# Where the steps that bring expert results home stand in a software pipeline

## The reference, cut to what matters

```python
x = _layernorm(x + linear_attention(x))          # softplus features, causal cumulative sums
x = _layernorm(x + cross_attention(x, ctx))      # 16 heads of 64, keys from 120 context rows and x
# the last sublayer, experts:
scores = softmax(x @ gate_w.T); topk_w, topk_i = top_k(scores, 2)      # 2 of 8 experts for each token
topk_w = topk_w / topk_w.sum(-1) * 2.5
y = sum over the two experts e of topk_w * (silu(x @ w_gate[e]) * (x @ w_up[e])) @ w_down[e]   # width 176
shared = (silu(x @ sw_gate) * (x @ sw_up)) @ sw_down                   # width 352, every token
x = _layernorm(x + y + shared)
```

## Time and profile before

| | us |
|---|---|
| median of 3 runs | 2102.3 (2101.9 to 2102.84) |
| the profiled execution's own time | 2103.97 |
| its span, first to last instruction | 2102.1 |
| PE, DVE, ACT, POOL busy | 1959.1, 1527.5, 1259.2, 1338.7 |
| mean granted TensorE clock | 0.974 of full |

### The profile page before, as it was taken

How to read it: one execution, slowest core, us unless ns; L and a number is a source line. 1 busy time by engine, 2 the same in 40 slices (tenths; PEclk the granted TensorE clock), 3 DMA queues, 4 the chain that set the end, 5 groups by cost and what they waited for, 6 DMA issues and landing times. The chain is left out here.

```text
span 2102.1 us, 47412 instructions
## 1 busy us (share of the span) xinstructions
PE 1959.1 (93%) x15991; PEld 1697.7 (81%) x15991; DVE 1527.5 (73%) x4030; ACT 1259.2 (60%) x3812; POOL 1338.7 (64%) x1475
## 2 busy tenths in 40 slices
PE   6888859999999999999999999999999989999874
PEld 4555448999999999999999999998999877888763
DVE  5999946777777777777777777778777755555554
ACT  4565526666666666666666666666666644444453
POOL 5899937566666666666666666666666664444564
PEclk9999969999999999999999999999999999999976
DMA  5200000000000000000000000001000022322344
GB/s 141 58 18 18 16 25 6 9 14 22 16 17 14 22 15 17 15 18 17 18 15 14 21 17 15 15 21 33 19 15 14 21 60 75 85 73 74 96 141 120
DMA packets 105022, 75.78 MB, mean 36 GB/s; under 512 B 11044, under 2 KB 98676, under 8 KB 104660
## 3 DMA queue, kind: packets, MB, share of 16 engines
q1 hardware_dynamic: 93732, 53.66, 9.4%
q0 software_dynamic: 8640, 17.97, 2.5%
q10 hardware_dynamic: 2416, 1.12, 0.2%
HBM read 40.15 MB, written 32.57 MB: 35 GB/s over the span
## 5 line engine op out<-in xcount | busy, mean ns | idle before, releaser
L1026 POOL TENSOR_TENSOR x_prob<-x_prob,x_inv 128x496 f32<-128x496 f32 x514 | 521.8, 1015 | 464.2 <-DVE x_inv L1176 461.7
L1104 ACT ACTIVATE x_prob<-x_ps_S,x_nmax 128x248 f32<-128x248 f32 x1028 | 472.8, 467 | 225.7 <-DVE x_nmax L1170 223.8
L1170 DVE TENSOR_REDUCE x_nmax<-x_ps_S 128x2 f32<-128x496 f32 x515 | 345.0, 670 | 106.0 <-PE x_ps_S L848 98.2
L1118 ACT COPY x_probT<-x_ps_T 124x512 f32<-124x512 f32 x512 | 300.3, 587 | 166.8 <-PE x_ps_T L1358 164.2
L846 PE MATMUL x_ps_S<-x_kT_lo,x_G_hi 128*128 128x248 f32 x1030 | 328.9, 319 | 0.0
L1358 PE MATMUL x_ps_T<-ident,x_prob 128*124 128x128 f32 x2048 | 319.4, 278 | 7.8 <-POOL x_prob L1026 6.3
L1358 PEld LDWEIGHTS x_ps_T<-ident,x_prob 128*124 128x124 f32 x2048 | 233.5, 140 | 74.0 <-POOL x_prob L1026 30.0
L848 PE MATMUL x_ps_S<-x_kT_hi,x_G_hi 128*128 128x248 f32 x1030 | 286.1, 278 | 0.0
L847 PE MATMUL x_ps_S<-x_kT_hi,x_G_lo 128*128 128x248 f32 x1030 | 286.0, 278 | 0.0
L1328 PE MATMUL x_ps_O<-x_probT,x_V 124*64 124x128 f32 x4096 | 251.9, 276 | 0.4 <-ACT x_probT L1118 0.4
L1585 POOL DMA_INDIRECT sorted_results<-e_y,w_wkv x142 | 145.1, 1022 | 164.9 <-DVE e_y L1717 153.4
(11 more groups left out here) (239 smaller groups left out, 4478.7 us busy)
## 6 DMA issues: line engine op xcount, KB each, us to landing
w_wkv<-sorted_rows SPq DMA_DIRECT2D x142, 66.0 KB
e_back<-sorted_results SPq DMA_DIRECT2D x28, 256.0 KB, 3.7
x_nk<-latents SPq DMA_DIRECT2D x34, 124.0 KB
latents<-lin_nlat SPq DMA_DIRECT2D x32, 128.0 KB, 1.8
turned_rows<-w_rows SPq DMA_DIRECT2D x32, 128.0 KB, 1.7
w_wq<-turned_rows SPq DMA_DIRECT2D x32, 128.0 KB
out_dram<-e_result SPq DMA_DIRECT2D x16, 256.0 KB, 2.8
x_nk<-in_ctx SPq DMA_DIRECT2D x34, 120.0 KB, 2.3
```

Of the source, the lines that this page charges most:

```text
L1026: nc.gpsimd.tensor_tensor(prob[:, k], prob[:, k], inv[:, k].unsqueeze(2).broadcast_to([P, 2, K]), ALU.mult).then_inc(prob_ready, 1)
L1104: nc.scalar.activation(prob[:, k, h, :], ps_S[:, n % BANKS, h * K:(h + 1) * K], ACT.Exp, bias=nmax[:, k, h:h + 1], accum_out=total[:, k, h ...
L1118: nc.scalar.copy(probT[0:KT, s % (2 * GANG)], ps_T[0:KT, s % 2, :]).then_inc(probT_ready, 1)
L1170: nc.vector.tensor_reduce(nmax[:, k, :], ps_S[:, n % BANKS, 0:2 * K].rearrange("p (h k) -> p h k", h=2), AX, ALU.max, negate=True).then_in ...
```

## The change

In `experts`:
- `add_pair` of group g moves to iteration 112 + 3g for g = 0 to 11 (12 groups in the block loop, not 9), and to 155, 157, 159 and 161 for groups 12 to 15. All loops are lengthened to STEPS_ALL = 170 iterations, and nothing is left behind them.
- SP's `load_back` of groups 0 to 11 moves to iteration 107 + 3g (five before `add_pair`; it was eight before), and SP's store to eight after `add_pair`. Groups 12 and 13 are loaded by SP in iteration 147, 14 and 15 by ACT in iteration 153.
- DVE's statistics are split over two iterations (`add_back`, `moments`), ACT's normalising over two (`normalise(g, pair)`). The addition of epsilon goes from POOL to DVE; POOL's power (`root`) stands in another iteration than `add_pair`, and ahead of it in the order.
- The shared groups 14 and 15 take seven iterations each from t = 143.

In `cross_attention` POOL makes the constants ahead of the first context rows.

```diff
-            for n in range(2):
-                context_deviation(n)
...
             nc.gpsimd.iota(ids[:], [[B * S, 2], [S, B]], base=0, channel_multiplier=1).then_inc(set_ready, 1)
...
             nc.gpsimd.tensor_tensor(before[:], tri[:], ident[:], ALU.subtract).then_inc(set_ready, 1)
+            for n in range(2):
+                context_deviation(n)
...
-    FIRST_BACK = FIRST_BLOCK[1] + 11
-    BACK_EVERY = 3
-    BACK = 9
+    LATE_FROM = TOTAL + 1
     WHOLE = FIRST[1] // GROUP
+    BACK_TIME = [FIRST_BLOCK[1] + 9 + 3 * g if g < WHOLE else TOTAL + 13 + 2 * (g - WHOLE) for g in range(GROUPS)]
+    STEPS_ALL = BACK_TIME[-1] + 9
...
+        def back_at(t, *delays):
+            for g, start in enumerate(BACK_TIME):
+                if t - start == delays[g >= WHOLE]:
+                    return g
+            return None
...
-                g = back_at(t + 8, 0)
-                if g is not None:
+                g = back_at(t, -5, -5)
+                if g is not None and g < WHOLE:
                     if g == 0:
                         sent_after(sp, FIRST_BLOCK[1])
                     for c in range(2):
                         load_back(sp, g, c)
-                g = back_at(t, 7)
+                if t == TOTAL + 5:
+                    sent_after(sp, TOTAL)
+                    for g in (WHOLE, WHOLE + 1):
+                        for c in range(2):
+                            load_back(sp, g, c)
+                g = back_at(t, 8, 7)
                 if g is not None:
                     store(g)
...
                 if 0 <= i < TOTAL:
                     scatter(i)
-                for delay, what in ((0, add_pair), (3, deviation)):
-                    g = back_at(t, delay)
-                    if g is not None:
-                        what(g)
+                g = back_at(t, 4, 3)
+                if g is not None:
+                    root(g)
+                g = back_at(t, 0, 0)
+                if g is not None:
+                    add_pair(g)
...
+                if t == TOTAL + 11:
+                    sent_after(act, TOTAL)
+                    for g in (WHOLE + 2, WHOLE + 3):
+                        for c in range(2):
+                            load_back(act, g, c)
```

More of the change, by code:

```diff
@@ L1074, in _ @@
             nc.gpsimd.tensor_tensor(before[:], tri[:], ident[:], ALU.subtract).then_inc(set_ready, 1)
+            for n in range(2):
+                context_deviation(n)
+                for u in range(2):
+                    normalise_context(n, n, u)
+                if n == 0:
+                    keys_hi(0, 0)
+                    keys_lo(0, 0)
             for k in range(2):
@@ L1456, in experts @@
         mom = room.sbuf("mom", [P, DEEP, GROUP, 2])
-        vare = room.sbuf("vare", [P, GROUP])
+        vare = room.sbuf("vare", [P, DEEP, GROUP])
         rstd = room.sbuf("rstd", [P, DEEP, GROUP])
@@ L1504, in shared_at, with prepared_at @@
         def shared_at(t):
-            g, k = divmod(t - SHARED_FROM, PIECES)
-            return (g, k) if 0 <= g < GROUPS else (None, None)
-        def back_at(t, delay):
-            g, rest = divmod(t - delay - FIRST_BACK, BACK_EVERY)
-            return g if rest == 0 and 0 <= g < BACK else None
+            if t >= LATE_FROM:
+                g, k = divmod(t - LATE_FROM, PIECES - 1)
+                g += GROUPS - LATE
+            else:
+                g, k = divmod(t - SHARED_FROM, PIECES)
+                if g >= GROUPS - LATE:
+                    return None, None
+            return (g, k) if 0 <= g < GROUPS else (None, None)
+        def prepared_at(t):
+            starts = [SHARED_FROM + PIECES * g for g in range(GROUPS)]
+            return starts.index(t) if t in starts else None
+        def back_at(t, *delays):
[3 more added lines that the diff above has]
+            return None
         @block.sync
@@ L1539, in _ @@
             slots.store_turned(sp, LAST)
-            for t in range(TOTAL + 4):
+            for t in range(STEPS_ALL):
                 if t % SET == 0 and t + RING < TOTAL:
                     load_rows(t // SET + LOADS)
-                g, k = shared_at(t + 13)
-                if g is not None and g > 1 and k == 0:
+                g = prepared_at(t + 13)
+                if g is not None and g > 1:
                     load_all(g)
@@ L1593, in add_pair, with root @@
                                         ).then_inc(pair_ready, 1)
-            def deviation(g):
+            def root(g):
                 wait(pool, shift_ready, g - DEEP + 1)
-                wait(pool, rstd_ready, g)
-                pool.wait_ge(mom_ready, (g + 1) * GROUP)
-                nc.gpsimd.tensor_scalar(vare[:], mom[:, g % DEEP, :, 1], EPS, None, ALU.add).then_inc(vare_ready, 1)
                 pool.wait_ge(vare_ready, g + 1)
-                nc.gpsimd.tensor_tensor(rstd[:, g % DEEP], vare[:], slots.half[:], ALU.pow).then_inc(rstd_ready, 1)
-            for t in range(TOTAL + 4):
+                nc.gpsimd.tensor_tensor(rstd[:, g % DEEP], vare[:, g % DEEP], slots.half[:], ALU.pow).then_inc(rstd_ready, 1)
+            for t in range(STEPS_ALL):
                 i = t - 3
@@ L1653, in all_gate, with normalise @@
                                      ).then_inc(all_silu_ready, 1)
[L1655 to L1659, removed]
+            def normalise(g, pair):
+                if pair == 0:
+                    act.wait_ge(shift_ready, g + 1)
+                    wait(act, stored[g % DEEP], g // DEEP * 16)
+                for k in (pair * 2, pair * 2 + 1):
                     nc.scalar.activation(result[:, g % DEEP, k, :], hsum[:, g % DEEP, k, :], ACT.Identity,
@@ L1671, in _ @@
                 g, k = shared_at(t)
-                if g is not None and g < GROUPS - LATE and k < NS:
+                if g is not None and k < NS:
                     all_gate(g, k)
-                g, k = shared_at(t + 2)
-                if g is not None and k == 0:
+                g = prepared_at(t + 2)
+                if g is not None:
                     all_hi(g)
@@ L1680, in _ @@
                     slots.scores_of(act, LAST)
[L1681 to L1692, removed]
+                for pair in range(2):
+                    g = back_at(t, 6 + pair, 5 + pair)
+                    if g is not None:
+                        normalise(g, pair)
+                if t == TOTAL + 11:
[3 more added lines that the diff above has]
+                            load_back(act, g, c)
         @block.vector
@@ L1749, in add_back, with moments @@
                 dve.wait_ge(sum_ready, g + 1)
-                for k in range(GROUP):
+                for k in range(2):
+                    v.bn_stats(stat[:, k, :], hsum[:, g % DEEP, k, :]).then_inc(stat_ready, 1)
+            def moments(g):
+                for k in range(2, GROUP):
                     v.bn_stats(stat[:, k, :], hsum[:, g % DEEP, k, :]).then_inc(stat_ready, 1)
@@ L1754, in add_back @@
                     v.bn_aggr(mom[:, g % DEEP, k, :], stat[:, k, :]).then_inc(mom_ready, 1)
+                dve.wait_ge(mom_ready, (g + 1) * GROUP)
+                wait(dve, rstd_ready, g - DEEP + 1)
+                v.tensor_scalar(vare[:, g % DEEP], mom[:, g % DEEP, :, 1], EPS, None, ALU.add).then_inc(vare_ready, 1)
             def shifts(g):
@@ L1769, in _ @@
                 g, k = shared_at(t)
-                if g is not None and g < GROUPS - LATE and k < NS:
+                if g is not None and k < NS:
                     all_product(g, k)
-                g, k = shared_at(t + 2)
-                if g is not None and k == 0:
+                g = prepared_at(t + 2)
+                if g is not None:
                     all_lo(g)
-                g, k = shared_at(t - PIECES + 1)
-                if g is not None and g < GROUPS - LATE and k == 0:
+                g, k = shared_at(t - 1)
+                if g is not None and k == PIECES - 2:
                     add_shared(g)
@@ L1781, in _ @@
                     slots.table(dve, 1, t - TABLE_AT)
-                g = back_at(t, 1)
+                g = back_at(t, 1, 1)
                 if g is not None:
                     add_back(g)
-                g = back_at(t, 5)
+                g = back_at(t, 2, 2)
+                if g is not None:
+                    moments(g)
+                g = back_at(t, 5, 4)
                 if g is not None:
                     shifts(g)
[L1788 to L1804, removed]
         @block.tensor
@@ L1884, in _ @@
                 g, k = shared_at(t)
-                if g is not None and g < GROUPS - LATE:
+                if g is not None:
                     shared(g, k)
```

21 lines of the change are left out of this document (removed).

## The result

| | before | changed |
|---|---|---|
| median us | 2102.1 (2099.61 to 2102.84, 4 runs) | 2116.18 (2114.67 to 2118.09, 4 runs) |
| profiled execution: own time, span | 2103.97, 2102.1 | 2114.67, 2112.9 |

The ratio is 1.007, 95% interval 1.0052 to 1.0087: slower by 14.1 us, where 2113.4 (+11.1) was forecast. The two profiled spans are 10.8 us apart.

A forecast was written before the change was run, and what follows sets the result against it. POOL's scatters and add_pair clock the loop (8.33 us a group); changed, a closed loop through the load would take 11.5. Terms: +35.1 loop, -19.2 tail, -4.8 constants = +11.1, so 2113.4 us, range 2098 to 2129.

The forecast's parts named there:

- Constants first: Start of cross attention: with constants moved into POOL's idle time, PE starts at about 300.5, not 305.31; -4.8 us.
- The closed loop: Block loop: scatter, landing, three row loads, two load_backs, landing, add_pair, scatter; 11.5 us a group, last scatter +35.1 us.
- the same gate: Block loop: the scatter of POOL's iteration 113+3g, right behind add_pair(g), gates the next load.
- the signs named: Block loop: add_pair of groups 1 to 8 each idle 4 to 6 us for the DMA; 11 to 13 us between add_pairs.
- The bounds of the period: Block loop: closed-loop period between 10.5 and 13.5 us a group, around the forecast 11.5.
- the first term: Closed loop, scatter to SP's row loads: 3.2 us, the quiet value and a little.
- the quiet stretch: Kernel before, around 1950 to 1962: scatter to row loads 2.95 and 2.98 us, against 4.46 in the busy stretch.
- The tail: Last scatter to end of the span: 28.0 us against 47.2 before, so -19.2, give or take 5.
- the chain that I gave: Tail: shared pieces 12 us, ACT's load of groups 14 and 15 landing at 18.6, add_pair through normalise 25.2, end 28.0.
- 3 us of slack: Tail: were the load's landing 3 us shorter, DVE's queue of four groups would end last.
- Rival 1: Block loop: load lands in time, engines set 6.7 us a group; 2066, chance 0.12 with its half-way form.
- Rivals 2 and 3: Block loop at its shortest, period 10.6, 2106, chance 0.13; with loaded DMAs, period 13.3, 2127, chance 0.20.

The follow-up runs named there:

- e1: The kernel before with only GpSimd's constants moved ahead of the first context rows: 2101.67 us, ratio 0.9978 to the kernel before.
- e10: e6 with all four late groups loaded by SP (iteration 147) and none by ACT: 2075.32 us, ratio 0.9859 to the kernel before.
- e11: e3 repeated unchanged, on another chip: 2075.89 us, ratio 0.9864 to the kernel before.
- e6: e3 with groups 12 and 13 taken before the last shared group and ACT's loads sooner: 2074.01 us, ratio 0.9871 to the kernel before.
- e3: The changed kernel with load_back of groups 0 to 11 three iterations sooner in SP's order: 2075.83 us, ratio 0.986 to the kernel before.
- e2: The kernel before with add_pair two iterations sooner and load_back at 107 + 3g, nothing split or spread: 2145.2 us, ratio 1.0189.
- e7: The changed kernel with load_back one iteration sooner in SP's order (106 + 3g): 2116.35 us, ratio 1.0077 to the kernel before.

## Why the prediction was right, point by point

**Constants first.** Forecast -4.8, PE at 300.5; in the trace PE is at 300.11 (-5.2), and the stretch of cross attention is 6.2 us shorter (5.9 in e1). The 6.75 at iteration 104 hold some 0.5 us more from behind that stage. Over all thirteen traces the move is worth 5.8 us, so the term was a microsecond small. The idle time is 5.0 of it; beside that the traces show another clock. Busy time by window, first before, then changed (us, PE, PEld, DVE, ACT, POOL, clock):

```profile
300.00:320.00 20.00, 10.64 (x56) 8.90 (x56) 7.24 (x15) 4.89 (x17) 6.33 (x35) 0.76 0.00 0
```

```profile
300.00:320.00 20.00, 16.01 (x98) 13.82 (x98) 10.51 (x22) 8.80 (x29) 8.36 (x11) 0.87 0.00 1
```

e1:

```profile
300.00:320.00 20.00, 15.46 (x92) 13.22 (x93) 10.74 (x24) 8.33 (x28) 7.53 (x9) 0.85 0.00 1
```

The granted clock is 0.87 and 0.85, not 0.76, in these 20 us. Of the ten traces with the move, the two with the lowest clock there (e10 0.76, e11 0.80) have the longest stretches (1367.2 and 1367.3, 4.8 us under the mean of the three without it), the eight at 0.81 to 0.87 have 1365.7 to 1366.4. That fits the clock as what gives the last microsecond, but it stays my reading: nothing was run that holds the one and changes the other.

**The closed loop.** It is there as described: the same gate, nine waits, the same order. Its terms over the eight turns: scatter to row loads 3.06 to 3.74, middle 3.42 (3.2 forecast); row loads 2.6; `load_back` to `add_pair` 3.95 to 4.3 in six turns and 5.08 and 5.48 in two (4.2); `add_pair` 1.26; to the scatter 0.15. The single turns are 10.54 to 13.42 us, the waits 3.07 to 6.25, both a little wider than the signs named. From the scatter of iteration 112 to `add_pair(0)` it is 6.8 us (6.5), from group 0 to 8 95.8, 12.0 a group (94.7), from there to the last scatter 17.8 (19.2). Together +35.1, as forecast; the mechanism is right, but that the sum agrees to the tenth is luck, since the misses of +0.3, +1.1 and -1.4 cancel. (The bounds of the period were summed loosely too: by their own terms they are 10.7 and 13.9, not 10.5 and 13.5.)

The Trainium skill's rule in "DMA: Bandwidth & Descriptors", section "Latency and other measured facts", that a DMA's fixed part shrinks under a lighter load, had been weighed for the first term; counted from the end of the scatter's instruction, the row loads come 1.98 to 2.02 us later in seven turns and 2.31 in the last, where the quiet stretch has 1.98 and 2.01 and the busy one 3.50. So the trace agrees, the quiet value held in the loop; the middle is 3.42 and not 2.95 because the scatter behind `add_pair` takes 1.43 us, not 0.97.

**The tail.** 29.65 us, 28.0 forecast, but not by the chain that I gave. I let ACT's load of groups 14 and 15 land last; no `add_pair` of theirs waited for it at the end. It was the other one, to which I had given only 3 us of slack. Changed kernel, PE and DVE:

```profile
2090.12 0.50 PE L846 MATMUL e_ps_gate<-e_all_lo,w_shared_gate_hi 128*128 128x512 f32 x1 [1.44 <-ACT e_all_silu L1656]
...
2094.40 2.94 PE L1859 MATMUL e_ps_s<-w_shared_down,e_all_hidden 128*128 128x128 f32 x24 [0.83 <-DVE e_all_hidden L1734]
```

```profile
2097.38 0.69 DVE L1742 TENSOR_TENSOR X<-X,e_ps_s 128x512 f32<-128x512 f32 x1 [1.91 <-PE e_ps_s L1859]
...
2099.02 0.69 DVE L1749 TENSOR_TENSOR e_hsum<-e_back,X 128x512 f32<-128x512 f32 x1
...
2101.86 0.69 DVE L1749 TENSOR_TENSOR e_hsum<-e_back,X 128x512 f32<-128x512 f32 x1
...
2104.69 0.69 DVE L1749 TENSOR_TENSOR e_hsum<-e_back,X 128x512 f32<-128x512 f32 x1
```

DVE waits 1.91 us for the last shared product with group 12's statistics queued behind it in order, and then takes the last groups at 2.84 us each. So that 28.0 came near is luck: it was summed along a chain that did not end last. e6 and e10, which move two groups ahead of the last shared product, gain at most a microsecond, because that product is then late by nearly as much.

**The rivals.** Rival 1 named the right switch: a load that is there in time. e3 gives it, 7.1 us a group (6.7 forecast) and a ratio of 0.986, which is 2073 by the 2102.3 that the prediction starts from, 7 us over its 2066 (its own median, 2076, is from another chip); its tail is 29.6 (28), and its loop has the slower first two turns. Rivals 2 and 3 were sizes of the same loop. What I said of the clock was too strong: from 1975 to 2064 it was 0.70, not well under.

**What was left.** The median moved by 14.1 us, the profiled span by 10.8. The difference is in which executions were profiled: the one of the kernel before (2103.97) took 1.9 us more than its median, the one of the changed kernel (2114.67) 1.5 us less than its own and is the fastest of its four. So the sum's agreement with the spans, +11.1 to +10.8, is partly luck; against the medians it is 3 us small.

## What to carry to other kernels

In a pipeline written out by iteration numbers, find for each load what it really waits for, and count the distance from there to its first use; the number at which it is issued says nothing by itself (one iteration sooner did nothing, three took 2.1% off). When a consumer moves ahead, ask whether something behind it in its engine's order is what releases its own next input: if so the whole latency becomes the period. A change that loses may hold a gain: here a load three iterations sooner turns 0.7% slower into 1.4% faster.

## What the runs showed of the hardware beyond that

- Taking 5.0 us of PE's idle time away shortened cross attention by 5.8 us on average (ten traces with the move 4.8 to 6.4 us under the mean of three without it), with the granted clock from 300 to 320 us at 0.76 to 0.87, where it was 0.74 to 0.76.
- From the end of a scatter's instruction on POOL to the first row load that SP issues behind its landing it is 1.98 to 2.02 us, in the quiet stretch of before and in the drained loop, and 3.50 in a busy stretch.
- With the loop drained, PE's clock from 1976 to 2040 us was 0.72 (0.76 in e2 and e7); before it was 0.83, and where the load is in time 0.97 (e3) and 0.89 (e11, the same kernel).
- The same kernel before had medians of 2102.1, 2106.7, 2102.8 and 2103.5 us in the four places where it ran beside the others; they lie further apart than several of the effects here are large.
